# Third pass of a two-layer gated attention kernel: rounding moved to VectorE, transposes two pairs ahead, four PSUM banks each for transposed norms and products

## The reference

```python
mu = jnp.mean(x, axis=-1, keepdims=True)
var = jnp.mean(jnp.square(x - mu), axis=-1, keepdims=True)
xn = (x - mu) * jax.lax.rsqrt(var + EPS) * gamma + beta
scale = jnp.maximum(jnp.max(jnp.abs(xn)), 1e-8) / 127.0     # over all batches
xq = jnp.round(jnp.clip(xn / scale, -127.0, 127.0)) * scale
wq = alpha * sign(w) * (abs(w) > delta)                     # ternary weights
x = x + jnp.tanh(g_ffn[1]) * einsum('bsi,oi->bso', xq, wq)
```

## Time and profile before

| What | us |
|---|---|
| median of 3 runs | 3008.16 |
| the profiled execution, its time | 3008.19 |
| its span in the profile | 3006.2 |
| busy over the span: TensorE matmul, VectorE, ScalarE, GpSimd | 2519.7, 2110.6, 1789.5, 1487.8 |
| first instruction of the third pass | 2827.01 |
| last addition of the third pass starts | 3002.50 |

### The profile page before, as it was taken

The page is one execution under the profiler, slowest core; times in us unless marked ns, Lnnn a source line. Parts: engine busy times, 40 slices in busy tenths (PEclk is TensorE's granted clock), DMA queues, the critical chain, the costliest instruction groups (busy, mean ns, idle before and its releaser), DMA issues. The chain is left out here.

```text
span 3006.2 us, 82393 instructions
## 1 busy us (share of the span) xinstructions
PE 2519.7 (84%) x28184; PEld 1800.6 (60%) x28184; DVE 2110.6 (70%) x6142; ACT 1789.5 (60%) x3015; POOL 1487.8 (49%) x2143
## 2 busy tenths in 40 slices
PE   3767777777777765999999999999999999999566
PEld 2445455555545544777777777777777777777344
DVE  4666666666666665778777877787778778878344
ACT  2666666666666663666566666665666666656355
POOL 2555555555555553444444544444444444444377
PEclk9998989899899997999999999999999999999756
DMA  2101111011110100000000000000000000000023
GB/s 68 33 29 31 31 31 31 28 31 31 31 31 28 32 14 17 18 19 18 19 19 16 21 17 18 19 18 19 19 19 18 16 19 19 18 19 13 22 101 102
DMA packets 99578, 82.87 MB, mean 28 GB/s; under 512 B 14928, under 2 KB 99280, under 8 KB 99280
## 3 DMA queue, kind: packets, MB, share of 16 engines
q1 hardware_dynamic: 99280, 78.88, 8.7%
HBM read 61.02 MB, written 16.78 MB: 26 GB/s over the span
## 5 line engine op out<-in xcount | busy, mean ns | idle before, releaser
L906 DVE TENSOR_REDUCE nmax<-bank_max 128x8 f32<-128x1024 f32 x256 | 312.6, 1221 | 371.5 <-DVEq L905 371.5
L617 ACT ACTIVATE stk<-bank_t 128x1024 bf16<-128x1024 bf16 x384 | 390.7, 1017 | 122.4 <-PE bank_t L1189 122.0
L649 ACT ACTIVATE stk<-bank_exp 128x1024 f32<-128x1024 f32 x256 | 262.0, 1023 | 201.7 <-ACTq L648 197.7
L622 ACT ACTIVATE probs<-bank_exp 128x512 f32<-128x512 f32 x512 | 288.8, 589 | 156.7 <-PE bank_exp L1169 156.7
L875 DVE TENSOR_REDUCE nmax<-bank_max 128x4 f32<-128x512 f32 x512 | 349.4, 683 | 31.9 <-PE bank_max L1156 31.7
L1218 PE MATMUL bank_max<-parts,QK 32*128 32x256 f32 x2048 | 333.2, 448 | 1.5 <-PEq L1281 1.5
L1225 PE MATMUL bank_exp<-parts,QK 32*128 32x256 f32 x2048 | 307.8, 421 | 0.0
L1189 PE MATMUL bank_t<-ident,parts 128*128 128x128 bf16 x4096 | 294.0, 220 | 2.6 <-PEq L1340 2.1
L487 POOL TENSOR_TENSOR rstd_f<-stat_f,eps_col 128x1 f32<-128x1 f32 x128 | 24.4, 191 | 522.5 <-POOLq L561 522.5
L1189 PEld LDWEIGHTS bank_t<-ident,parts 128*128 128x128 bf16 x4096 | 252.5, 98 | 21.6 <-issue 3.0
L1351 PE MATMUL bank_m<-wT,QK 128*128 128x256 f32 x1024 | 252.7, 391 | 1.2 <-PEq L1347 1.2
(11 more groups left out here) (181 smaller groups left out, 6647.5 us busy)
## 6 DMA issues: line engine op xcount, KB each, us to landing
X<-in_x SPq DMA_DIRECT2D x128, 128.0 KB, 2.1
stk<-in_ctx SPq DMA_DIRECT2D x128, 128.0 KB, 2.1
QK<-in_ctx SPq DMA_DIRECT2D x128, 128.0 KB, 2.1
out_y<-X SPq DMA_DIRECT2D x64, 256.0 KB, 2.1
ff_qq<-in_mask_BxSxS_ik SPq DMA_DIRECT2D x128, 64.0 KB, 1.9
stk<-shift_T SPq DMA_DIRECT2D x128, 8.0 KB
X<-in_L_xattn_Wq SPq DMA_DIRECT2D x1, 256.0 KB, 6.9
X<-in_L_xattn_Wk SPq DMA_DIRECT2D x1, 256.0 KB, 7.2
```

Source lines behind the costliest of these rows:

```text
L617: nc.scalar.activation(stk[k2][:, :, g * HG:(g + 1) * HG, :].rearrange("p w h t -> p w (h t)"), bank_tb[bank].rearrange("p (w n) -> p w n" ...
L622: nc.scalar.activation(probs[g % 2][:, :, :], bank_exp[g % 2][:, :, :], ACT.Exp, scale=SCALE).then_inc(probs_made, 1)
L649: nc.scalar.activation(a_probs[n], exp_pair[:, :, :, :].rearrange("p i h t -> p (i h) t"), ACT.Exp, scale=SCALE).then_inc(probs_made, 1)
L906: return v.tensor_reduce(nmax[:, n * H // 2:(n + 1) * H // 2], max_pair[:, :, :, :].rearrange("p i h t -> p (i h) t"), axis=AX.X, op=ALU.m ...
```

## The change

The rounding of a pair is done by VectorE in place of GpSimd, as the first instruction of its step, ahead of the addition of the pair before; GpSimd has nothing left in this pass. The transposes run two pairs ahead of the product in place of one, and go to a ring of four banks `bank_x`: the two `bank_t`, and `bank_o` and `bank_m`, which this pass did not use. Centring runs three pairs ahead in place of two. `c_f` has four slots, which fill all of `stk[1]`, and `c_qT` four slots, in the `QK` tiles. ScalarE does its eviction first and then its centring. VectorE's order in a step is rounding of pair i, addition of pair i - 1, centring of pair i + 3. TensorE's is transposes of pair i + 2, product of pair i.

```diff
--- before.py
+++ after.py
@@ -164,9 +164,10 @@
 
         c_x = [stk[0][:, :, :, :].rearrange("p w h t -> p (w h t)").bitcast(FP32)[:, n * 2 * D:(n + 1) * 2 * D]
                for n in range(RING)]
-        c_f = [stk[1][:, 0, n * 8:(n + 1) * 8, :].rearrange("p h t -> p (h t)").bitcast(FP32)
-               .rearrange("p (c b t) -> p c b t", c=DC, b=2) for n in range(2)]
-        c_qT = [stk[1][:, 1, n * 4:(n + 1) * 4, :].rearrange("p (c b) t -> p c b t", c=DC) for n in range(2)]
+        c_f = [stk[1][:, :, :, :].rearrange("p w h t -> p (w h t)").bitcast(FP32)[:, n * 2 * D:(n + 1) * 2 * D]
+               .rearrange("p (c b t) -> p c b t", c=DC, b=2) for n in range(RING)]
+        c_qT = [t[:, 0:2, :, :].rearrange("p g w n -> p (g w n)").bitcast(BF16)
+                .rearrange("p (c b t) -> p c b t", c=DC, b=2) for t in QK]
         c_shift = absmax
         gb_T = sb("gb_T", [P, 2, DC], FP32)
         mask_t = [ff_q[n].bitcast(I32) for n in range(2)]
@@ -185,6 +186,7 @@
         bank_m = ps("bank_m", [P, 512], FP32)
         bank_tb = [b[:, :].bitcast(BF16) for b in bank_t]
         bank_y = [b.rearrange("p h t -> p (h t)") for b in bank_max + bank_exp]
+        bank_x = [b[:, :] for b in (*bank_t, bank_o, bank_m)]
         bank_mb = bank_m[:, :].bitcast(BF16)
         bank_xb = [b.rearrange("p h t -> p (h t)").bitcast(BF16) for b in bank_max]
 
@@ -587,18 +589,6 @@
             pool.drain().then_inc(pass_ends[1], 1)
             pool.wait_ge(pass_ends[1], 5)
 
-            def step_c(k):
-                pool.wait_ge(fq_out, 1)
-                pool.sem_inc(fq_out, -1)
-                nc.gpsimd.tensor_scalar(c_qT[k % 2].rearrange("p c b t -> p (c b t)"),
-                                        c_f[k % 2].rearrange("p c b t -> p (c b t)"), ROUND, ROUND,
-                                        ALU.add, ALU.subtract).then_inc(fq_made, 1)
-
-            with pool.Fori(0, NB // 2 - RING + 1, RING):
-                for k in range(RING):
-                    step_c(k)
-
-
         @block.scalar
         def _(act):
             act.wait_ge(consts_in, 16 * 16)
@@ -741,19 +731,19 @@
             act.wait_ge(pass_ends[1], 5)
 
             def step_c(i, k, live):
-                if live(2):
-                    nc.scalar.activation(c_x[(k + 2) % RING][:, 0:D], xs(2 * i + 4), ACT.Identity,
-                                         bias=col(c_shift, 2 * i + 4), scale=col(rstd4, 2 * i + 4))                      .then_inc(c_centred, 1)
                 if live(0):
                     act.wait_ge(fq_T, 1)
                     act.sem_inc(fq_T, -1)
                     for c in range(DC):
-                        last = nc.scalar.activation(c_f[k % 2][:, c, :, :],
-                                                    bank_t[k % 2][:, :].rearrange("p (b c t) -> p c b t", b=2, c=DC)[:, c],
+                        last = nc.scalar.activation(c_f[k][:, c, :, :],
+                                                    bank_x[k].rearrange("p (b c t) -> p c b t", b=2, c=DC)[:, c],
                                                     ACT.Identity, bias=gb_T[:, 1, c:c + 1], scale=gb_T[:, 0, c:c + 1])
                     last.then_inc(fq_out, 1)
-
-            steps_c(step_c, -2, NB // 2, C_FIRST, C_LAST, act)
+                if live(3):
+                    nc.scalar.activation(c_x[(k + 3) % RING][:, 0:D], xs(2 * i + 6), ACT.Identity,
+                                         bias=col(c_shift, 2 * i + 6), scale=col(rstd4, 2 * i + 6))                      .then_inc(c_centred, 1)
+
+            steps_c(step_c, -3, NB // 2, C_FIRST, C_LAST, act)
 
 
         @block.vector
@@ -1105,16 +1095,21 @@
 
             def c_step(i, k, live):
 
+                if live(0):
+                    vec.wait_ge(fq_out, 1)
+                    vec.sem_inc(fq_out, -1)
+                    v.tensor_scalar(c_qT[k].rearrange("p c b t -> p (c b t)"), c_f[k].rearrange("p c b t -> p (c b t)"),
+                                    ROUND, ROUND, ALU.add, ALU.subtract).then_inc(fq_made, 1)
                 if live(-1):
                     vec.wait_ge(fy_made, 1)
                     vec.sem_inc(fy_made, -1)
                     v.scalar_tensor_tensor(xs_pair(2 * i - 2), bank_y[(k + 3) % RING],
                                            nmax[:, 4:5], xs_pair(2 * i - 2), ALU.mult, ALU.add).then_inc(x_done, 1)
-                if live(2):
-                    v.tensor_scalar(c_x[(k + 2) % RING][:, D:2 * D], xs(2 * i + 5), col(rstd4, 2 * i + 5),
-                                    col(c_shift, 2 * i + 5), ALU.mult, ALU.add).then_inc(c_centred_v, 1)
-
-            steps_c(c_step, -2, NB // 2 + 1, C_FIRST, C_LAST, vec)
+                if live(3):
+                    v.tensor_scalar(c_x[(k + 3) % RING][:, D:2 * D], xs(2 * i + 7), col(rstd4, 2 * i + 7),
+                                    col(c_shift, 2 * i + 7), ALU.mult, ALU.add).then_inc(c_centred_v, 1)
+
+            steps_c(c_step, -3, NB // 2 + 1, C_FIRST, C_LAST, vec)
 
 
         @block.tensor
@@ -1405,25 +1400,26 @@
             pe.wait_ge(pass_ends[1], 5)
 
             def step_c(i, k, live):
-                if live(1):
+                if live(2):
+                    s = (k + 2) % RING
                     pe.wait_ge(c_centred, 1)
                     pe.sem_inc(c_centred, -1)
                     pe.wait_ge(c_centred_v, 1)
                     pe.sem_inc(c_centred_v, -1)
                     for n in range(2 * DC):
-                        last = nc.tensor.transpose(bank_t[(k + 1) % 2][:, n * P:(n + 1) * P],
-                                                   c_x[(k + 1) % RING][:, n * P:(n + 1) * P], identf[:, :])
+                        last = nc.tensor.transpose(bank_x[s][:, n * P:(n + 1) * P], c_x[s][:, n * P:(n + 1) * P],
+                                                   identf[:, :])
                     last.then_inc(fq_T, 1)
                 if live(0):
                     pe.wait_ge(fq_made, 1)
                     pe.sem_inc(fq_made, -1)
                     y = bank_y[k % RING]
                     for n in range(2 * DC):
-                        last = mm(y[:, n // DC * D:(n // DC + 1) * D], c_qT[k % 2][:, n % DC, n // DC, :],
+                        last = mm(y[:, n // DC * D:(n // DC + 1) * D], c_qT[k][:, n % DC, n // DC, :],
                                   tern[:, n % DC, :], start=n % DC == 0, stop=n % DC == DC - 1)
                     last.then_inc(fy_made, 1)
 
-            steps_c(step_c, -1, NB // 2, C_FIRST, C_LAST, pe)
+            steps_c(step_c, -2, NB // 2, C_FIRST, C_LAST, pe)
 
 
 INPUTS = ['x', 'ctx_1024', 'mask_BxSxS2_ik1', 'g_xattn', 'g_ffn', 'L0_ffn_kernel', 'L0_ffn_input_scale',
```

## The result

The changed kernel takes 2925.31 us (median of 4 runs, 2925.04 to 2926.26) against 3008.68 of the kernel before beside it: a ratio of 0.9722, interval 0.9705 to 0.9739. The forecast was 2939 us with a range of 2926 to 2958.

What follows compares the result with a forecast made beforehand. The third pass was taken as bound by a chain of handovers through GpSimd's rounding, no engine full. Gains of 8.5 + 63 x (2.57 - 1.60) = 69.6 us off 3008.16 gave 2939 us, range 2926 to 2958.

Steps and rivals of the forecast that it cites:

- a loop of two steps: Third pass before the change: rounding, product, transposes and eviction close over two steps, 5.28 us, 2.64 for one.
- Rounding 0.43: Rounding moved to VectorE: taken as 0.43 us an instruction, like L969, where GpSimd needed 1.93.
- Centring 0.40: VectorE's centring in the third pass: 0.40 us with GpSimd empty, in place of 0.579 on average.
- Start 8.5 us: Start of the third pass: first addition at about 2832.1 in place of 2840.64, 8.5 us gained.
- ScalarE's 1.41 a step as the floor: ScalarE's eviction and centring in the third pass: 0.92 + 0.49 = 1.41 us, the least a step could last.
- The loop with 1.68 at the lower clock and 1.27 at the higher: Third pass after the change, through VectorE and TensorE: 3.36 or 2.53 us for two steps, by TensorE's clock.
- half and half gives 1.59; I take 1.60: Third-pass step expected with TensorE half the time at each clock: 1.59 us, taken as 1.60; chance 0.50.
- the 1.50 for the higher clock: Third-pass step expected while TensorE runs at 2.4 GHz: at least 1.41 us, taken as 1.50 with waits.
- the third, the clock high: Rival: TensorE's clock goes high and stays, ScalarE sets steps of 1.41 to 1.48, 2927 to 2931 us; chance 0.14.
- the low case: Rival: TensorE's clock stays low in the third pass, steps 1.68 to 1.9, 2944 to 2957 us; chance 0.23.
- The slower rival: Rival: rounding costs VectorE 1.93 us as on GpSimd, step 2.84, time 3018 us; chance 0.03.
- the rival without effect: Rival: a handover closes the same loop, step stays near 2.57, only the start is gained, 3000 us; chance 0.02.

Runs made afterwards that it cites:

- the loop opened alone: Changed kernel with the rounding left on GpSimd, keeping the longer look-ahead, four banks and four slots; 2971.80 us, 0.9864 of the kernel before.
- the 0.49 that came through whole: Changed kernel with ScalarE's centring issued twice a step, the copy to an unused tile; additions 1.89 us apart, 2959.32 us, one run.
- the kernel with the memset: Changed kernel plus a one-column memset on GpSimd right behind the meeting of the engines ahead of the third pass; 2926.39 us, one run.

## Why the prediction was wrong, step by step

- What bound the kernel before: rounding on GpSimd was on a loop of two steps, as stated; with the loop opened alone the step fell to GpSimd's 1.94. The other path of that kernel, through VectorE's order of centring behind addition, was not seen. It did not matter for the forecast of the full change.
- Rounding 0.43: measured 0.427. Centring 0.40: measured 0.405. Stores hidden: 2.1 us to landing as before. Start 8.5 us: measured 8.65. All right. The Trainium skill's rule (VectorE: DVE Perf Modes, the perf-mode tier table), two elements a cycle from SBUF and one from PSUM in float32, agrees with them again, 0.427 against 0.745 for the addition.
- ScalarE's 1.41 a step as the floor: measured 1.40, and it is the bound, shown by the 0.49 that came through whole.
- The loop with 1.68 at the lower clock and 1.27 at the higher: real, by the run with transposes doubled (1.48 calculated, 1.50 measured). At the high clock it is below ScalarE's 1.40.
- **The step that failed** is "half and half gives 1.59; I take 1.60". The clock was at 1.00 before the first addition and stayed there, so the term 1.68 had no share at all; and of the 1.50 for the higher clock the 0.09 "for waits that three nearly equal engines will still catch" did not exist: VectorE and TensorE waited in each step, and nothing was added to ScalarE's own 1.40. In numbers: 63 x (1.60 - 1.50) = 6.3 us for the clock, 63 x (1.50 - 1.40) = 6.3 for the waits, 1.1 for the last steps without centring, 13.7 in all. The unrounded forecast, 2938.6, less these 13.7 and the 0.15 at the start, plus the 1.72 by which the pass began later, is 2926.4; the profiled execution took 2926.26.
- The case that came true is the third, the clock high, with 0.14. "At that pace it is busy 0.83 of 1.41 us only" was no argument against it: with the same work in steps of 1.89 us the clock stayed at 1.00. The rows had shown only that it wavers with a step of 2.57, and I read a coin toss into that. Why the clock holds at the shorter steps stays open; what is shown is that it did.
- The rule of the Trainium skill (TensorE: Matmul & The Clock Gate, Part 4 on transposes) that transposes don't count for the clock as matmuls do spoke for the low case. What I drew from it is refuted: half of the matmuls are transposes, two thirds in one run, and the clock reads 1.00. Whether the rule itself holds isn't shown, because each step has products too.
- The range ended at 2926, just above the 2925.31 measured, because ScalarE's 1.41 was taken for all 63 steps; the last three lack the centring. A bound from the slowest engine's row sum has to be taken with the steps that lack part of the work.
- The slower rival and the rival without effect had no part in it.

## What to carry to other kernels

When several engines have nearly the same work a step, write down each one's sum of start-to-start distances and every loop with the number of steps it may take to close; the largest was the step here, to within 0.02 where ScalarE, VectorE or the loop set it, with no allowance on top. (Where TensorE did, it was 1.75 against 1.66.) A look-ahead of one more pair is worth what it takes from the loop it is in, down to the next bound, so look for the queued instruction (here a centring behind an addition) that carries the loop round. A clock that wavers in a half-idle stage is no forecast of it in the same stage made faster: give high and low a case each and don't average them.

## What the runs showed of the hardware

- The granted clock in the third pass over stretches of 20 us, the matmuls of a step being the same: 1.00 at steps of 1.40, 1.74 (from 2860 on) and 1.89 us, 0.83 to 1.00 at 1.95, 0.50 to 0.84 at 2.38, 0.50 to 0.73 at 2.58. In the changed kernel it was still 0.50 in 2828 to 2832, where TensorE began the pass after 16.8 us without a matmul.
- ScalarE's records grow along the pass although its work does not: the two-part eviction is 1.02 us long at 2830.80 and 1.57 at 2914.24, with starts 1.39 apart and ends 1.40. So "20.00 of 20" and a longer mean are no measure of its work; the distances of the starts are. What fills the longer records isn't shown.
- Who pays when VectorE and GpSimd work side by side differs: VectorE's centring was held to the end of GpSimd's rounding before (0.64 in the earlier trace rows), GpSimd's centring stretched from 0.55 to 0.98 with one a step, and with two a step VectorE's rounding (0.66) and GpSimd's second centring (0.71) were longer.
- GpSimd's all-reduce costs more than its 0.38 us: it starts about 5 us behind the end of the reduction that it waits for (5.1 in the kernel with the memset), and the next add-and-subtract came after 7.4 and 11.9 us without work, though a memset was on time.
